# Tiles 4 to 9 of x laid out transposed by the host, their means spread by TensorE and subtracted by VectorE, and four weight slices moved to SyncE's queue

## The chip, the cores and the metric

The kernel runs on one core of one Trainium2 chip. The metric is the device time of one execution in microseconds (us). The arithmetic is f32; each f32 operand of a large product is split into a high part in the fp32r format and a low part, and three products (high x high, high x low, low x high) are summed, so that precision is kept.

## The reference, cut to what matters

x has 1250 rows (nodes) of 1024 features; there are 41,250 edges of two relations. Two layers, each with a residual:

```python
h = relu(layernorm(x))                        # rows
n = lnw * h * rsqrt(mean(h * h) + 1e-6)
y = elu(n @ W_root + bias + sum_r mean_over_edges_r(n @ W_rel[r]))
x = x + h + y @ wo
h = relu(layernorm(x)) @ W_gat                # second layer
e = exp(-leaky_relu(h @ a_l [src] + h @ a_r [dst]))
x = x + elu(scatter_sum(e * h[dst]) / (scatter_sum(e) + 1e-5))
```

The part that the change touches is the left operand of `n @ [W_rel, W_root]`: relu(layernorm(x)), transposed.

## The kernel before

The rows of x are worked in ten tiles of 125 (`TILES`, `T`), the 1024 features in eight slices of 128 (`KT`). Each engine has its own program, and semaphores tie them together; `data(t)` is the count that a semaphore has when tile t's data are there, `room(t)` and `room1(t)` the counts at which a buffer or bank is free again. `pipeline` (L269) runs stages with lags, tile after tile. There is no scheduler: the order on each engine is what is written.

First stage (about 10 to 120 us). For tile t: SyncE loads the rows into `xt` (`load_x`, L298). VectorE takes mean and variance (`variance`, L896; `moments`, L892) and the reciprocal of the deviation (`deviation`, L906). ScalarE normalises and takes relu in one instruction into `ht` (`norm`, L499) and the root of the mean square (`mean_square`, L506). GpSimd adds h to x (`residual`, L436) and SyncE stores the sum (`store_xh`, L303). TensorE turns the eight slices of `ht` into two PSUM banks (`transposed`, L1350; 8 transposes), ScalarE copies them out as `hT_hi` (`transposed`, L519), VectorE takes the rest as `hT_lo` = PSUM - `hT_hi` (`low_parts`, L917). TensorE then makes 48 products of the tile (`products`, L1358, by `split_products`, L1324), which ScalarE and VectorE scale by `stats1[..., 5]` and split into messages (`messages`, L536 and L934). The last tile's products (`last_products`, L1400) are mixed with the first counting matmuls.

```python
            def stage1(first, end):                                                     # TensorE, L1390
                pipeline((transposed, 1), (products, 2), steps=(first, end))
            def stage1(first, end):                                                     # VectorE, L974
                pipeline((transposed, 1), (messages, 2), (moments, -1), steps=(first, end))
```

So in a step VectorE does the low parts of one tile, the messages of the tile before, and the moments of a tile ahead. Between its steps it prepares the edges, one piece per step (L997 to L1012): `quotients` (L830), `listed` (L836), `picks` (L844), `spans_of_windows` (L859), then `window_keys` (L877) and `first_rows` (L970). TensorE needs them in its own queue: `picked` (L1331) stands behind the products of tile 5 and waits for the picks, `windows_transposed` (L1338) behind those of tile 7, `total` (L1346) behind those of tile 8. GpSimd's gather (L453) waits for the spans, and tile 8's residual stands behind it.

The passage to the second layer (about 230 to 260 us). SyncE's loop over tiles (L376) stores tile t's x1, then loads tile t + 2 of x + h (`load_xh`, L345), which waits until the store of the same buffer has ended; slice 0 of the second layer's weights is in that loop too (L383). ScalarE issues slices 1 to 3 behind the copy of slice 0 (L763) and slices 4 to 7 behind a change of its function table (`back_to_exp`, L767), ahead of `turned(TILES - 1, 0)` (L770), the first copy of the last tile's counts out of PSUM. TensorE's third counts transposition of that tile (L1669) waits for this copy. ScalarE and VectorE split the slices into `wg` (L641, L1093), and the products of tile 0 take them one after another (`products2`, L1563).

## Time and profile before

| | us |
|---|---|
| median of three runs | 515.79 (515.06 to 517.19) |
| the profiled execution, whole | 514.97 |
| its span, first to last instruction | 513.2 |
| TensorE busy in it | 495.4 |
| VectorE, ScalarE, GpSimd busy | 374.9, 226.7, 74.7 |
| mean granted clock of TensorE | 0.998 |

The profile names an instruction by its line in the program, its engine (PE is TensorE, PEld its weight loads, DVE VectorE, ACT ScalarE, POOL GpSimd, SPq SyncE's queue) and by output <- inputs. Matmuls overlap one another, so what one costs its engine is the distance from its start to the next one's start. "idle before" is the time in which the engine had nothing to do before an instruction, and the arrow names whose work ended it.

### The profile page before, as it was taken

What the parts mean: (1) busy time and instruction counts of PE and PEld (TensorE: products, weight loads), DVE (VectorE), ACT (ScalarE), POOL (GpSimd) and SP (SyncE); (2) the same over time, 40 slices, a digit from 0 to 9 for tenths busy, and PEclk for the clock granted to TensorE, in tenths of its full rate; (3) what the DMA queues carried; (4) which work ended last, traced back from release to release, by engine and by line L of the source; (5) the groups of instructions that cost most, each with busy time, mean ns of one, the idle gap of its engine ahead of it and who ended that gap; (6) DMA issues with size and microseconds to landing.
All of it is one profiled execution on the core that took longest, in us unless ns stands there. A gap on an engine that the chain in (4) does not pass through costs nothing.

```text
span 513.2 us, 7812 instructions
## 1 busy us (share of the span) xinstructions
PE 495.4 (97%) x2983; PEld 426.2 (83%) x2983; DVE 374.9 (73%) x644; ACT 226.7 (44%) x382; POOL 74.7 (15%) x72
## 2 busy tenths in 40 slices
PE   3999999999999999999999999999999999999996
PEld 2889989988989988898788888888887888888886
DVE  4846885598889999997865555556598878777633
ACT  5865443415966666667632222224233333223211
POOL 1362213100000000000000000000083333322400
PEclk9999999999999999999999999999999999999999
DMA  9872273404013235247911111100022222222211
GB/s 259 228 239 81 80 228 117 127 1 114 2 47 112 84 99 143 81 123 277 319 53 40 41 41 41 41 0 0 1 80 82 83 90 69 81 80 81 70 53 44
DMA packets 22186, 49.15 MB, mean 96 GB/s; under 512 B 4798, under 2 KB 10709, under 8 KB 22018
## 3 DMA queue, kind: packets, MB, share of 16 engines
q1 hardware_dynamic: 20879, 44.66, 29.2%
q10 hardware_dynamic: 1008, 3.67, 2.0%
q8 instruction: 26, 0.43, 0.4%
q0 software_dynamic: 256, 0.26, 0.2%
q14 instruction: 17, 0.14, 0.1%
HBM read 33.05 MB, written 16.85 MB: 97 GB/s over the span
## 4 chain that ended last, share of the span: by engine, by line
PE 86%; DVE 7%; DMA 4%; ACT 2%; issue 1%; SPq 0%; ACTq 0%; DVEq 0%
PE ps L1328 11%; PE ps L1593 9%; PE ps L1595 9%; PE ps L1594 9%; PE ps L1487 8%; PE ps L1574 7%; PE ps L1575 7%; PE ps L1576 7%; PE ps L1397 4%; PE ps L1416 2%; DMA x_scratch<-xt 1%; PE ps L1546 1%; DMA xt<-xh_scratch 1%; PE ps L1560 1%; PE ps L1548 1%; PE ps L1547 1%
## 5 line engine op out<-in xcount | busy, mean ns | idle before, releaser
L1593 PE MATMUL ps<-h_hi,att_hi 125*125 125x512 f32 (+1 forms) x190 | 73.5, 387 | 0.0
L1594 PE MATMUL ps<-h_lo,att_hi 125*125 125x512 f32 (+1 forms) x190 | 72.6, 382 | 0.0
L1595 PE MATMUL ps<-h_hi,att_lo 125*125 125x512 f32 (+1 forms) x190 | 72.5, 382 | 0.0
L1574 PE MATMUL ps<-wg,gT_hi 128*125 128x512 f32 x160 | 63.8, 399 | 0.3 <-DVE wg L1097 0.3
L1575 PE MATMUL ps<-wg,gT_hi 128*125 128x512 f32 x160 | 63.1, 394 | 0.0
L1576 PE MATMUL ps<-wg,gT_lo 128*125 128x512 f32 x160 | 63.0, 394 | 0.0
L1487 PE MATMUL ps<-msg_hi,adj_hi 125*125 125x288 f32 x180 | 50.3, 303 | 0.2 <-ACT adj_hi L596 0.2
L1487 PE MATMUL ps<-msg_lo,adj_hi 125*125 125x286 f32 x180 | 45.9, 295 | 0.0
L471 POOL TENSOR_TENSOR some<-first_att 125x625 f32<-125x625 f32 x1 | 2.4, 2440 | 277.8 <-DVE first_att L1157 277.8
L691 ACT ACTIVATE em<-ps,rinv 125x512 f32<-125x512 f32 (+1 forms) x21 | 14.0, 669 | 64.2 <-DVE hp L1201 64.2
L1595 PEld LDWEIGHTS ps<-h_hi,att_lo 125*125 125x125 f32 x190 | 35.2, 186 | 7.9
L1594 PEld LDWEIGHTS ps<-h_lo,att_hi 125*125 125x125 f32 x190 | 35.2, 185 | 7.5
L1593 PEld LDWEIGHTS ps<-h_hi,att_hi 125*125 125x125 f32 x190 | 35.2, 185 | 7.4
L1328 PE MATMUL ps<-w_hi,hT_hi 128*125 128x430 f32 x112 | 40.7, 363 | 0.5 <-DVE hT_lo L920 0.5
L1328 PE MATMUL ps<-w_hi,hT_lo 128*125 128x430 f32 x112 | 40.1, 358 | 0.0
L1328 PE MATMUL ps<-w_lo,hT_hi 128*125 128x430 f32 x112 | 40.0, 357 | 0.0
L1135 DVE CUSTOM_DVE_ANT_0 h_lo<-ps,a_b 125x1024 fp32r<-125x1024 f32 x20 | 24.5, 1224 | 18.1 <-PE ps L1576 17.7
L1574 PEld LDWEIGHTS ps<-wg,gT_hi 128*125 128x125 f32 x160 | 29.7, 186 | 7.7 <-DVE wg L1097 0.7
L1576 PEld LDWEIGHTS ps<-wg,gT_lo 128*125 128x125 f32 x160 | 29.6, 185 | 7.3
L1575 PEld LDWEIGHTS ps<-wg,gT_hi 128*125 128x125 f32 x160 | 29.7, 186 | 6.9
L668 ACT CAST h_hi<-ps 125x1024 fp32r<-125x1024 f32 x10 | 10.2, 1016 | 55.4 <-DVE diag L1139 55.4
L596 ACT CAST adj_hi<-ps 125x500 fp32r<-125x500 f32 x45 | 26.7, 592 | 16.2 <-PE ps L1397 15.5
(215 smaller groups left out, 1116.6 us busy)
## 6 DMA issues: line engine op xcount, KB each, us to landing
xt<-in_x SPq DMA_DIRECT2D x10, 448.0 KB
xh_scratch<-xt SPq DMA_DIRECT2D x10, 448.0 KB
xt<-xh_scratch SPq DMA_DIRECT2D x10, 448.0 KB
x_scratch<-xt SPq DMA_DIRECT2D x10, 448.0 KB
x1t<-x_scratch SPq DMA_DIRECT2D x10, 448.0 KB
xr<-x_scratch SPq DMA_DIRECT2D x10, 448.0 KB
out_x<-xr SPq DMA_DIRECT2D x19, 224.0 KB
wg_raw<-in_L_gnn_W ACTq DMA_DIRECT2D x7, 512.0 KB, 7.4
```

Source lines behind the costliest of these rows:

```text
L596: A.copy(columns(adj_hi, b, g), bank_of).then_inc(S["win_out"], 1)
L691: A.activation(em[b][:, first:end], heads(b, h, (first, end)), ACT.Exp, scale=rinv[b][:, 0:1]).then_inc(S["el_rdy"], 1)
L1135: V.tensor_tensor_reduce(out=halves(h_lo[:, TILES - 1, :]), in0=hps, in1=halves(a_b[:, s, :]), scale=1.0, scalar=0.0, op0=ALU.mult, op1=AL ...
L1328: last = M.matmul(out, lhsT, rhs, start=(n == 0), stop=(n == len(terms) - 1))
L1397: last = M.matmul(win_bank(n, x), srcs, wide, start=c == 0, stop=c == SLOTS - 1)
L1487: last = M.matmul(*product, start=(s == 0 and n == 0), stop=(end and n == 1), skip_group_check=True)
L1574: M.matmul(to, hi, wg[k][:, 0, cut], start=n == 0, stop=False)
L1575: M.matmul(to, hi, wg[k][:, 1, cut], start=False, stop=False)
L1576: last = M.matmul(to, lo, wg[k][:, 0, cut], start=False, stop=n == KT - 1)
L1593: M.matmul(to, hi[:, s, :], h_hi[:, s, cut], start=s == 0, stop=False)
L1594: M.matmul(to, hi[:, s, :], h_lo[:, s, cut], start=False, stop=False)
L1595: return M.matmul(to, lo[:, s, :], h_hi[:, s, cut], start=False, stop=s == TILES - 1)
```

## The change

The host hands x over a second time as `x_turned`, ten tiles with the features along the partitions (128 x 8 x 125). SyncE loads tiles 4 to 9 of it into two new buffers `x_t` (`load_x_turned`). For these tiles TensorE no longer transposes `ht`. `means` multiplies the column of the tile's means, broadcast over 128 columns, by the identity: one matmul puts the mean of each row into every partition of a bank. VectorE subtracts it from `x_t` (`centred`), ScalarE takes relu of that as `hT_hi` (`high_parts`), and VectorE takes the low part from `x_t` and `hT_hi` (`turned_low_parts`). The rows are no longer scaled by the reciprocal deviation at this place; it goes into the factor of the messages (`mean_square`). `norm` and the sum x + h stay as they are. Tile 3 keeps its transposes. Apart from that, weight slices 4 to 7 are issued by SyncE ahead of `load_x1(2, 0)`, and no longer by ScalarE.

```diff
+    TURNED = 4
...
+    XT_AT = (2 * TILES * N - 2 * 4 * KT * T) // 32 * 32
...
+        turned_of = ExitStack()
+        sb(turned_of, "below_x_t", [P, XT_AT // 2], BF16)
+        x_t = [sb(turned_of, f"x_t{b}", [P, KT, T], F32) for b in range(2)]
+        turned_of.close()
...
+            def load_x_turned(t, b):
+                if t >= TURNED + 2:
+                    sp.wait_ge(S["hT_lo_rdy"], data(t - 2))
+                sp.dma_start(x_t[b][:], x_turned[t].rearrange("p (k n) -> p k n", n=T)).then_inc(S["xt_in"][b], 16)
...
             load_x(5, 1)
+            load_x_turned(4, 0)
+            load_x_turned(5, 1)
             store_xh(2, 0)
             store_xh(3, 1)
...
                 store_xh(t, t % 2)
                 if t + 2 < TILES:
                     load_x(t + 2, t % 2)
+                if TURNED + 2 <= t + 1 < TILES:
+                    load_x_turned(t + 1, (t + 1) % 2)
...
                 if t == TILES - 2:
+                    sp.wait_ge(S["s_ps"], data(TILES - 1))
+                    for k in range(4, KT):
+                        load_wg(k)
                     load_x1(2, 0)
                 store_x1(t, t % 2)
...
             def norm(t, b):
                 act.wait_ge(S["rstd_rdy"], data(t))
-                act.wait_ge(S["hT_ps"], room(t))
+                if t < TURNED + 2:
+                    act.wait_ge(S["hT_ps"], room(t))
                 act.wait_ge(S["xh_rdy"], room(t))
                 A.activation(ht[b][:], xt_of(t)[:], ACT.Relu, bias=stats1[:, bass.ds(t, 1), 3],
...
+            def high_parts(t, b):
+                act.wait_ge(S["centred"], t - TURNED + 1)
+                act.wait_ge(S["g_ps"], room(t))
+                A.activation(hT_hi[b][:], x_t[b][:], ACT.Relu).then_inc(S["hT_hi_rdy"], 1)
...
-            pipeline((transposed, 1), (messages, 2), (normed, -1), steps=(AHEAD, TILES + 1))
+            transposed(3, 1, 1)
+            for t in range(AHEAD, TILES):
+                messages(t - 2, t % 2, t // 2 - 1)
+                high_parts(t, t % 2)
+                if t + 1 < TILES:
+                    normed(t + 1, 1 - t % 2, (t + 1) // 2)
+            messages(TILES - 2, 0, TILES // 2 - 1)
...
                 if k == 1:
                     act.wait_ge(S["sum_16"], data(TILES - 1))
-                if k == 4:
-                    act.wait_ge(S["s_ps"], data(TILES - 1))
                 act.dma_start(wg_raw[k][:], w_gat[k * P:(k + 1) * P, :]).then_inc(S["wg_in"][k], 16)
...
                 back_to_exp()
-                for k in range(4, KT):
-                    load_wg(k)
                 turned(TILES - 1, 0)
                 elu(*last)
                 turned(TILES - 1, 1)
...
             def mean_square(t):
+
                 dve.wait_ge(S["rm_rdy"], data(t))
-                V.reciprocal(stats1[:, bass.ds(t, 1), 5], stats1[:, bass.ds(t, 1), 5]).then_inc(S["rms_rdy"], 1)
+                last = V.reciprocal(stats1[:, bass.ds(t, 1), 5], stats1[:, bass.ds(t, 1), 5])
+                if t >= TURNED:
+                    last.then_inc(S["rs1_rdy"], 1)
+                    dve.wait_ge(S["rs1_rdy"], t - TURNED + 1)
+                    last = V.tensor_tensor(stats1[:, bass.ds(t, 1), 5], stats1[:, bass.ds(t, 1), 5], stats1[:, bass.ds(t, 1), 2], ALU.mult)
+                last.then_inc(S["rms_rdy"], 1)
+
+            def centred(t, b):
+                dve.wait_ge(S["xt_in"][b], (t - b) * 8 + 16 - 8 * TURNED)
+                dve.wait_ge(S["mean_ps"], t - TURNED + 1)
+                V.tensor_tensor(x_t[b][:], x_t[b][:], bank(b, P, T).unsqueeze(1).broadcast_to([P, KT, T]), ALU.subtract).then_inc(S["centred"], 1)
+
+            def turned_low_parts(t, b):
+                dve.wait_ge(S["hT_hi_rdy"], data(t))
+                V.scalar_tensor_tensor(hT_lo[b][:], x_t[b][:], 0.0, hT_hi[b][:].bitcast(F32), ALU.max, ALU.subtract).then_inc(S["hT_lo_rdy"], 1)
...
-            def stage1(first, end):
-                pipeline((transposed, 1), (messages, 2), (moments, -1), steps=(first, end))
+            def step1(t):
+                centred(t, t % 2)
+                messages(t - 2, t % 2, t // 2 - 1)
+                turned_low_parts(t, t % 2)
+                mean_square(t)
+                if t + 1 < TILES:
+                    moments(t + 1, 1 - t % 2, (t + 1) // 2)
 
             dve.wait_ge(S["consts"], 1)
...
-            stage1(AHEAD, 5)
+            transposed(3, 1, 1)
+            step1(4)
             quotients()
-            stage1(5, 6)
+            step1(5)
             listed()
-            stage1(6, 7)
+            step1(6)
             picks()
-            stage1(7, 8)
+            step1(7)
             spans_of_windows()
-            stage1(8, 9)
-            stage1(9, 10)
+            step1(8)
+            step1(9)
             window_keys()
             first_rows(range(0, 2))
-            stage1(10, 11)
+            messages(TILES - 2, 0, TILES // 2 - 1)
             missing()
             first_rows(range(2, 2 * NG))
-            stage1(11, 12)
+            messages(TILES - 1, 1, TILES // 2 - 1)
...
+            def means(t):
+
+                b = t % 2
+                pe.wait_ge(S["var_rdy"], data(t))
+                if t >= TURNED + 2:
+                    pe.wait_ge(S["centred"], t - TURNED - 1)
+                else:
+                    pe.wait_ge(S["hT_lo_rdy"], data(TURNED - 1 if TURNED < AHEAD else TURNED - 2))
+                M.matmul(bank(b, P, T), mv[b][:, 0:1].broadcast_to([T, P]), ident[0:T, 0:T], start=True, stop=True).then_inc(S["mean_ps"], 1)
+
             def stage1(first, end):
-                pipeline((transposed, 1), (products, 2), steps=(first, end))
+                for t in range(first, end):
+                    products(t, t % 2, t // 2)
+                    if t + 2 < TILES:
+                        means(t + 2)
...
-            stage1(AHEAD, 8)
+            transposed(3, 1, 1)
+            stage1(2, 6)
             picked()
-            stage1(8, 10)
+            stage1(6, 8)
             windows_transposed()
-            stage1(10, 11)
+            stage1(8, 9)
             total()
             last_products()
...
+    laid = {name: inputs[name] for name in INS}
+    laid["x_turned"] = np.asarray(inputs["x"]).reshape(10, 125, 8, 128).transpose(0, 3, 2, 1).reshape(10, 128, 1000)
+    for name in [INS[0], "x_turned"] + INS[1:]:
+        a = np.ascontiguousarray(laid[name])
```

VectorE, the step ahead of the picks (`picks` begins at the CAST into `qb`); `hT_lo` is a tile's low parts, `bn` and `mv` the moments of tile 7. Before:

```order
L920 TENSOR_TENSOR hT_lo<-ps,hT_hi 128x500 x2
L932 RECIPROCAL stats<-stats 125x1
L943 SCALAR_TENSOR_TENSOR root<-ps,stats,bias_b 125x286
L945 SCALAR_TENSOR_TENSOR msg_lo<-ps,stats,msg_hi 125x572
L823 BN_STATS bn<-xt 125x6 x2
L904 BN_AGGR mv<-bn 125x2
L908 RECIPROCAL stats<-stats 125x1
L910 SCALAR_TENSOR_TENSOR stats<-mv,stats 125x1
L848 CAST qb<-quot 110x3x125
```

Now:

```order
L969 TENSOR_TENSOR x_t<-x_t,ps 128x1000
L984 SCALAR_TENSOR_TENSOR root<-ps,stats,bias_b 125x286
L986 SCALAR_TENSOR_TENSOR msg_lo<-ps,stats,msg_hi 125x572
L973 SCALAR_TENSOR_TENSOR hT_lo<-x_t,hT_hi 128x1000
L959 RECIPROCAL stats<-stats 125x1
L963 TENSOR_TENSOR stats<-stats 125x1
L849 BN_STATS bn<-xt 125x6 x2
L930 BN_AGGR mv<-bn 125x2
L934 RECIPROCAL stats<-stats 125x1
L936 SCALAR_TENSOR_TENSOR stats<-mv,stats 125x1
L874 CAST qb<-quot 110x3x125
```

The centring stands at the head of the step, the low parts have moved behind the messages, and a second scale instruction has come; all of it is ahead of the picks. The low parts in this step were tile 5's and are tile 6's now, the messages are tile 4's in both.

TensorE, the end of tile 5's products (L1328, now L1375) and what follows. Before:

```order
L1328 MATMUL ps<-w_lo,hT_hi 125x430
L1328 MATMUL ps<-w_hi,hT_lo 125x430
L1335 MATMUL ps<-qb,pick 125x127 x6
L1355 MATMUL ps<-ident,ht 128x125 x8
L1328 MATMUL ps<-w_hi,hT_hi 125x430
```

Now:

```order
L1375 MATMUL ps<-w_lo,hT_hi 125x430
L1375 MATMUL ps<-w_hi,hT_lo 125x430
L1445 MATMUL ps<-ident,mv 128x125
L1382 MATMUL ps<-qb,pick 125x127 x6
L1375 MATMUL ps<-w_hi,hT_hi 125x430
```

The matmul that spreads a mean (tile 7's here) comes before the six of `picked`, and tile 6's products follow them at once; the eight transposes are gone.

ScalarE in the passage, from the table change on. Before:

```order
L576 ACT_TABLE_LOAD
L576 ACTIVATE ssq<-eps 125x1
L639 DMA wg_raw<-in_L_gnn_W 128x1024 x4
L616 CAST counts<-ps 125x500
L621 ACTIVATE eb<-eb 125x286
```

Now:

```order
L684 ACTIVATE x1t<-x1t,stats 125x1024
L607 ACT_TABLE_LOAD
L607 ACTIVATE ssq<-eps 125x1
L647 CAST counts<-ps 125x500
L652 ACTIVATE eb<-eb 125x286
```

The four DMAs have left the place ahead of the copy of counts; in SyncE's queue they stand between the load of tile 9 of x + h and that of `x1t` for tile 2.

## Rows read from the trace of the kernel before

**Rows 1.** The page's busy table: engine, busy us, share of span, instructions.

```profile
PE 495.4 (97%) x2983; PEld 426.2 (83%) x2983; DVE 374.9 (73%) x644; ACT 226.7 (44%) x382; POOL 74.7 (15%) x72
```

**Rows 2.** Waits of TensorE: engine, line, for whom, us in total, times, longest.

```profile
PE ps L1514 <- ACT counts L616: 1.0, 1, 1.0
...
PE ps L1574 <- DVE wg L1097: 0.3, 1, 0.3
```

**Rows 3.** Timeline of TensorE: start us, busy us, line, output<-inputs, form, count.

```profile
44.10 1.02 PE L1355 MATMUL ps<-ident,ht 125*128 125x125 f32 x8
44.88 0.43 PE L1328 MATMUL ps<-w_hi,hT_hi 128*125 128x430 f32 x1
...
54.38 1.04 PE L1355 MATMUL ps<-ident,ht 125*128 125x125 f32 x8
```

**Rows 4.** Timeline of TensorE at 282 us, second layer.

```profile
282.34 0.38 PE L1584 MATMUL ps<-diag,ones 125*125 125x125 f32 x2
282.56 0.91 PE L1560 MATMUL ps<-ident,x1t 125*128 125x125 f32 x7
```

**Rows 5.** Timeline of VectorE, 45 to 75 us, first stage.

```profile
45.07 0.52 DVE L943 SCALAR_TENSOR_TENSOR root<-ps,stats,bias_b 125x286 f32<-125x286 f32 x1 [1.94 <-ACT msg_hi L539]
...
46.22 1.28 DVE L823 BATCH_NORM_STATS2 bn<-xt 125x6 f32<-125x512 f32 x2
...
48.49 0.74 DVE L832 CAST edges_f<-edges_i 110x1125 f32<-110x1125 int32 x1
...
49.66 0.36 DVE L828 TENSOR_SCALAR quot<-quot 110x375 f32<-110x375 f32 x1
50.05 2.50 DVE L827 TENSOR_SCALAR quot<-edges_f 110x375 f32<-110x375 f32 x1
...
52.97 1.26 DVE L920 TENSOR_TENSOR hT_lo<-ps,hT_hi 128x500 fp32r<-128x500 f32 x2
...
58.70 0.54 DVE L838 SCALAR_TENSOR_TENSOR comb<-quot,edges_f 110x375 f32<-110x375 f32 x1
...
63.57 1.26 DVE L920 TENSOR_TENSOR hT_lo<-ps,hT_hi 128x500 fp32r<-128x500 f32 x2
...
69.11 0.55 DVE L848 CAST qb<-quot 110x375 bf16<-110x375 f32 x1
...
74.84 1.25 DVE L920 TENSOR_TENSOR hT_lo<-ps,hT_hi 128x500 fp32r<-128x500 f32 x2
```

**Rows 6.** Timeline of GpSimd, the residual of tile 5.

```profile
49.94 2.40 POOL L438 TENSOR_TENSOR xt<-ht,xt 125x1024 f32<-125x1024 f32 x1 [9.18 <-ACT ht L503]
```

**Rows 7.** Groups of VectorE by line and form: count, busy us, mean ns, idle.

```profile
L1153 DVE SCALAR_TENSOR_TENSOR first_att<-first_att 125x1000 f32<-125x1000 f32 x1 | 1.2, 1199 | 0.0
```

**Rows 8.** Timeline of TensorE, the picks' matmuls and tile 6's products.

```profile
75.22 0.51 PE L1335 MATMUL ps<-qb,pick 110*125 110x127 bf16 x6
...
77.05 0.44 PE L1328 MATMUL ps<-w_hi,hT_hi 128*125 128x430 f32 x1
```

**Rows 9.** Timeline of TensorE, its first matmuls.

```profile
8.68 1.93 PE L1385 MATMUL ps<-ident,ht 125*128 125x125 f32 x8 [3.26 <-ACT ht L503]
...
12.92 1.02 PE L1355 MATMUL ps<-ident,ht 125*128 125x125 f32 x8
```

**Rows 10.** Stretches after TensorE's end: length, busy us by engine, granted clock, DMA.

```profile
508.50:509.00 0.50, 0.28 (x3) 0.07 (x1) 0.18 (x1) 0.00 (x0) 0.00 (x0) 1.00 0.07 10
...
511.00:511.50 0.50, 0.00 (x0) 0.00 (x0) 0.00 (x0) 0.00 (x0) 0.00 (x0) 0.71 0.50 141
```

**Rows 11.** Timeline of ScalarE, the copy of the last tile's counts.

```profile
238.48 0.58 ACT L616 CAST counts<-ps 125x500 uint16<-125x500 f32 x1 [1.27 <-issue]
```

**Rows 12.** Chain that ended last, 234 to 249 us: start, us, what.

```profile
234.30 7.49 DMA x_scratch<-xt
...
242.15 7.01 DMA xt<-xh_scratch
```

**Rows 13.** The weight slices' DMAs: us to landing, shortest, median, longest.

```profile
DMA to landing us min/median/max: 3.6/7.0/10.2
```

10 lines of the change are left out of this document (4 added, 6 removed).

## The prediction

> **What bounds the kernel now.** I read the page's busy table first. TensorE is busy for 495.4 of 513.2 us [rows 1], so almost every microsecond of its queue is on the path, and a change pays only by taking work or waits out of that queue. Then I asked who TensorE waits for [rows 2]: once it has started, its waits are short, and two of them lie where this change works: 1.0 us for a ScalarE copy of counts and 0.3 us for the last slice of the second layer's weights. So I read two places as timelines. In the first stage (34 to 108 us) TensorE goes from tile to tile without a gap; VectorE has about as much to do there, because four pieces of edge preparation (quotients, list, picks, spans) stand between its tiles. In the passage from the first layer to the second (234 to 257 us) the chain of waits leaves TensorE and runs through a store, a load and VectorE.
>
> One execution was profiled: 514.97 us, of which 513.2 are the span. The median of the three runs is 515.79. The sum below is a difference, worked out on the profiled execution and added to the median. A measurement of this kernel can tell about 0.5% (2.6 us) from no change.
>
> **TensorE, per tile.** For tiles 4 to 9 the eight transposes go. They begin at 44.10 and the next product begins at 44.88 [rows 3]: 0.78 us. What comes in their place is one small matmul with a broadcast operand. The nearest row is the matmul that spreads the diagonal in the second layer, 0.22 us from start to start [rows 4]. That leaves 0.56 us a tile, 3.4 us over six, if nothing else ends later. A tile's 48 products take 9.50 us (44.88 to 54.38) [rows 3], so the period falls from 10.28 to 9.72 us.
>
> **VectorE, per tile.** Before, a step is low parts (two instructions), messages, moments. Now it is centring, messages, low parts, two tiny scale instructions, moments. Prices from the rows of this stage: messages 1.15 us (45.07 to 46.22), moments 2.27 (46.22 to 48.49) [rows 5]. The new low part has two operands of 1000 columns in SBUF; the same instruction on 125x1000 took 1.20 us [rows 7], of which the start of the next overlaps a little: 1.15. The centring has one operand in PSUM; no row shows it with a broadcast, and by the 1000 columns of [rows 7] it lies between 1.1 and 1.3: 1.15. Scales 0.27. Sum 6.0 us, where the step before had 4.8. The 1.2 us more are hidden only while VectorE has slack in that period, and it has none in three steps in a row: after tile 4 the quotients follow (48.49 to 52.97, 4.48 us), after tile 5 the list (58.70 to 63.57, 4.87), after tile 6 the picks (69.11 to 74.84, 5.73) [rows 5].
>
> Followed through: the mean of tile 4 is spread when the products of tile 2 end, so step 4 starts at about 44.4. It ends with its quotients at 44.4 + 6.0 + 4.48 = 54.9. Step 5 with the list ends at 54.9 + 6.0 + 4.87 = 65.8. Step 6 with the picks ends at 65.8 + 6.0 + 5.73 = **77.5**, where it ended at 74.84 before. The centring stands at the head of VectorE's step, so messages, low parts, moments and the preparation all queue behind it.
>
> Who waits for the picks: TensorE's six `picked` matmuls, which stand behind the products of tile 5, as before. TensorE now gets there earlier: 44.10 + 0.22, then three periods of 9.50 and 0.22, is 73.5 us. It waits **4.0 us**, where before it came at 75.22 and found the picks done [rows 8]. It can't go round them: the products of tile 6 stand behind `picked` in its queue. They start at 77.5 + 0.5 = 78.0 instead of 77.05 [rows 8], 0.9 us late. All that tiles 4 to 7 had won is gone. Tiles 8 and 9 give back 2 x 0.56. The first stage ends **0.2 us earlier**. By an error of 0.1 us in each of the six new large instructions this is off by 0.6 either way.
>
> Covered, with the cover named. The low parts of tile 7 are done at 77.5 + 3.5 = 81, and its products can't start before 87.5; tiles 8 and 9 have more. The window keys come 2 us closer to their use and still before it. ScalarE loses 2 copies of 500 columns and gains one of 1000. SyncE's queue takes six more loads of 500 KB; the tightest is tile 8's, which stands behind the list's spans and tile 9's rows; it is wanted at 88, and low parts 6 us later still come before TensorE asks for them.
>
> **The clock.** TensorE's last matmul ends at 508.78; the granted clock is still full until 511 and 0.71 in the half microsecond after it, so it fell to its lower level (1.2 of 2.4 GHz) about 2.4 us after the engine stopped [rows 10]. A stop of 4.0 us in mid-kernel is longer. What it costs is read from the start, where TensorE came out of idleness: eight transposes took 1.93 us at 8.68, and the next eight, at 12.92, 1.02 [rows 9]. So the price is between 0.9 us (those transposes alone) and 2.1 (half of the 4.2 us in between); no row decides, and I take 1.2, nearer the lower, since the level may rise before 12.92. The Trainium skill, "TensorE: Matmul & The Clock Gate", section "HAM oscillation", speaks against this change in the same way: a matmul kernel that idles between bursts comes back at half rate each time. By that the gain of the change is eaten here; without it the sum is 1.2 us lower.
>
> **The passage to the second layer.** ScalarE issued the four slices itself, and the copy of counts behind them starts at 238.48 after 1.27 us of "issue" [rows 11]. TensorE waits 1.0 us for that copy [rows 2]. With the issues gone the copy runs at 237.2; TensorE goes on at 238.0 with eight transposes and then waits for y of the last tile, which needs ScalarE's exponential of the same stretch and comes 0.6 us earlier. So of 1.0 us, **0.6** stays. SyncE issues the slices behind its load of tile 9, and that load waits for the store of tile 7, which took 7.49 us; the load then took 7.01 and landed at 249.16 [rows 12], with slices on the other queue moving beside both. Without four of them the store ends no later and the load has the engines for itself; in half its time it would be there at 245.7, and VectorE would no longer wait for it. Its splits then run 1 to 2 us ahead, and the **0.3** us [rows 2] that TensorE stood at the last slice goes too. Sum **0.9 us earlier**; between 0, if the slices now come late, and 1.3, all of both waits.
>
> **The sum:** -0.2 - 0.9 + 1.2 = +0.1; 515.79 + 0.1 = **515.9 us**, no change that can be measured. Nothing later in the kernel depends on either place except through TensorE's queue.
>
> **Rivals.**
> 1. *The clock stays up.* For it: one fall in the trace, at the end, isn't a rule for a stop of 4 us, and the small matmul of the mean and the six of the picks fall near its ends. Then the sum is -1.1: 514.7 us.
> 2. *VectorE is in time.* If its step were short enough for the picks at 73.5, TensorE would save all: products of tile 6 at 74.0 instead of 77.05, then 1.1, then 0.9: -5.05, 510.7 us. Against it: 4 us would have to be missing from 35 us of VectorE rows. It decides from picks before 75 us.
> 3. *VectorE meets GpSimd.* GpSimd's residual add starts at 49.94 and takes 2.40 us [rows 6]. The VectorE instruction that runs into it, at 50.05, took 2.50 us, where the one before it, of the same kind and shape, took 0.36 [rows 5]: 2.1 us lost. Before, low parts read one operand from PSUM; now both are in SBUF. If the add falls on them in steps 4 to 6, the picks come 3 x 2.1 = 6.3 us later still, and all of that is TensorE's: 522 us. Against it: the add begins 1.45 us after the moments end and is over by 3.9, in the middle of the preparation, while the next low part starts at 6.8 at the earliest; it decides if the add is delayed by 3 us. Only tile 8's, which stands behind the gather, can meet one, with 5 us of slack. The Trainium skill, "SBUF — State Buffer", section "Who interferes with whom", has the rule: a VectorE instruction with two SBUF inputs is blocked in full by a GpSimd one that reads SBUF. By that rule alone each new low part is at risk; by the rows none on the path is.
> 4. *The slices come late.* One took 10.2 us to land at most [rows 13]; issued at 244.1 it would land at 254.3, be split by 256.5, with ScalarE's and VectorE's copies: TensorE would go on when it did before, and of the 0.9 us nothing is left, 516.8 us. Against it: four slices of 512 KB alone on the engines have no rival traffic but one load.
>
> **Chances.** The forecast, stall and slow clock, 0.45 (515.9, and 515 to 517 by its bounds). The stall without the clock 0.25 (514.7). VectorE in time, or the stall under 2 us, 0.14 (510.7 to 513). GpSimd or another delay of over 2.6 us 0.11. Late slices 0.05. Faster by over 0.5% means below 513.2: 0.16, with a little from the second case's lower end. Slower by over 0.5%, above 518.4: 0.12. Within: 0.72. The range runs from 510.5 to 518.5: it takes in rival 2, and leaves out the GpSimd case and little more.
>
> **What would show it.** Right: VectorE's picks end near 77.5; TensorE shows one wait of 3.5 to 4.5 us on them; the granted clock is below 1 around 76 to 80 and the products there take twice as long; the first stage's last products start within 0.5 us of before, plus what the clock cost; the wait on the counts copy is gone. Wrong: picks before 75 us, a low part of over 2 us, a centring over 1.4, or TensorE waiting on `x_t` loads or on the slices.

## The result and the profile after

| | before | changed |
|---|---|---|
| median of six runs each | 515.94 | 518.93 (517.64 to 519.32) |
| ratio to before | 1 | 1.0049, interval 1.0035 to 1.0064 |
| the profiled execution, whole | 514.97 | 518.34 |
| its span | 513.2 | 516.1 |
| mean granted clock | 0.998 | 0.995 |

The changed kernel is slower by 0.49%, 2.5 us (1.8 to 3.3). The forecast was 515.9 with a range of 510.5 to 518.5; 1.0049 x 515.79 is 518.3, inside the range by 0.2 us (the changed kernel's own median of 518.93 is above it). "No change that can be measured" holds by a hair only: the loss is under the 0.5% that the forecast named, but it is clear of the noise, and the forecast's middle was 2.4 us too low. The first stage came out as forecast and the passage did not, so that the time still fell into the range is partly luck.

TensorE's busy time in the page fell as it should, and the span grew:

```profile
PE 492.4 (95%) x2947; PEld 424.0 (82%) x2947; DVE 382.3 (74%) x650; ACT 227.4 (44%) x376; POOL 74.7 (14%) x72
```

That is 3.0 us less work [rows 1] and 2.9 us more span. TensorE's waits (engine, line, for whom, us in total, times, longest) say where the work's place was taken:

```profile
PE ps L1382 <- DVE pick L882: 4.3, 1, 4.3
...
PE ps L1635 <- DVE wg L1144: 2.0, 1, 2.0
```

The first is the stall that the forecast named. The second is 2.0 where it was 0.3 [rows 2], and the forecast had it gone. The wait of 1.0 on the counts [rows 2] is gone; 0.6 us on y, behind it, is what was left of it.

**First stage.** VectorE's timeline of the changed kernel (start, busy us, line, output<-inputs, form, count): a step with the quotients behind it (L853), one with the list (L867), and the step with the picks (L879, L882).

```profile
44.27 1.20 DVE L969 TENSOR_TENSOR x_t<-x_t,ps 128x1000 f32<-128x1000 f32 x1 [0.99 <-PE ps L1445]
...
46.57 1.20 DVE L973 SCALAR_TENSOR_TENSOR hT_lo<-x_t,hT_hi 128x1000 fp32r<-128x1000 f32 x1
...
51.00 0.35 DVE L853 TENSOR_SCALAR quot<-edges_f 110x375 f32<-110x375 f32 x1
...
51.78 2.51 DVE L853 TENSOR_SCALAR quot<-edges_f 110x375 f32<-110x375 f32 x1
...
54.72 1.20 DVE L969 TENSOR_TENSOR x_t<-x_t,ps 128x1000 f32<-128x1000 f32 x1
...
62.41 2.63 DVE L867 SCALAR_TENSOR_TENSOR comb<-comb,edges_f 110x375 f32<-110x375 f32 x1
...
65.54 1.19 DVE L969 TENSOR_TENSOR x_t<-x_t,ps 128x1000 f32<-128x1000 f32 x1
...
73.02 2.94 DVE L879 TENSOR_SCALAR below<-iw,last_q 110x250 bf16<-110x250 f32 x3
75.99 1.26 DVE L882 SCALAR_TENSOR_TENSOR pick<-iw,most,below 110x250 bf16<-110x250 f32 x3
77.17 1.19 DVE L969 TENSOR_TENSOR x_t<-x_t,ps 128x1000 f32<-128x1000 f32 x1
```

Centring and low part take 1.20 us each and 1.1 from start to start. Step 4 with the quotients lasts 10.45 (44.27 to 54.72; forecast 10.48), step 5 with the list 10.82 (10.87), step 6 with the picks 11.63 (11.73). The picks end at 77.2. TensorE, a tile's period and the stall:

```profile
43.91 0.44 PE L1375 MATMUL ps<-w_hi,hT_hi 128*125 128x430 f32 x1
...
53.35 0.38 PE L1445 MATMUL ps<-ident,mv 125*128 125x125 f32 x2
53.49 0.44 PE L1375 MATMUL ps<-w_hi,hT_hi 128*125 128x430 f32 x1
...
72.61 0.38 PE L1445 MATMUL ps<-ident,mv 125*128 125x125 f32 x2
77.30 0.90 PE L1382 MATMUL ps<-qb,pick 110*125 110x127 bf16 x6 [4.31 <-DVE pick L882]
77.97 0.70 PE L1375 MATMUL ps<-w_hi,hT_hi 128*125 128x430 f32 x1
78.47 0.56 PE L1375 MATMUL ps<-w_lo,hT_hi 128*125 128x430 f32 x1
...
88.65 0.38 PE L1445 MATMUL ps<-ident,mv 125*128 125x125 f32 x2
```

This tile takes 9.58 us (43.91 to 53.49), where the forecast had 9.72 and the kernel before 10.28: the mean's matmul costs 0.14 here, not 0.22, and the 48 products of tile 3 took 9.44, not 9.50. Over all six tiles the transposes cost 0.77 to 0.81 us each before, and the means cost 0.14 to 0.22: about 0.62 us saved per tile. TensorE had spread the mean of tile 7 by 73.0, waited 4.31 us, and did tile 6's products in 10.68 us (77.97 to 88.65) where 9.50 is the full-clock time [rows 3]. The picks' matmuls took 0.67 us from the first to the products behind them; at full clock they take 0.37 (the run with a filler, below). The clock beside it, in stretches of 1 us (length, busy us of PE, PEld, DVE, ACT, POOL with instructions, granted clock, DMA share, GB/s):

```profile
76.00:77.00 1.00, 0.00 (x0) 0.00 (x0) 1.00 (x3) 0.00 (x0) 0.00 (x0) 1.00 1.03 359
77.00:78.00 1.00, 0.70 (x7) 0.70 (x7) 1.00 (x2) 0.00 (x0) 0.00 (x0) 0.55 1.05 361
...
79.00:80.00 1.00, 1.00 (x5) 0.91 (x4) 1.00 (x2) 0.42 (x1) 0.00 (x0) 0.50 0.99 383
...
81.00:82.00 1.00, 1.00 (x7) 0.95 (x6) 1.00 (x2) 0.00 (x0) 0.00 (x0) 1.00 0.13 53
```

The clock is at half speed (1.2 GHz) from shortly before TensorE resumes until about 80.5.

**The passage.** The chain of waits of the changed kernel (start, us, what):

```profile
245.63 10.10 DMA x1t<-x_scratch
...
255.82 1.30 DVE bn L849 x2
...
257.46 1.10 DVE wg L1144
```

Before, the chain went through the load of tile 9 of x + h [rows 12]. Now it goes through SyncE's queue (four slices are issued from 243.06 on) to the load of x1 for tile 2 behind them, 10.10 us, then VectorE's moments of that tile, then the last slice's split, then TensorE. Two more views:

ScalarE's timeline, the changed kernel:

```profile
237.89 0.56 ACT L647 CAST counts<-ps 125x500 uint16<-125x500 f32 x1
...
254.64 1.05 ACT L672 CAST wg<-wg_raw 128x1024 fp32r<-128x1024 f32 x1 [1.50 <-DMA wg_raw<-in_L_gnn_W]
```

VectorE's timeline, the changed kernel:

```profile
255.82 1.29 DVE L849 BATCH_NORM_STATS2 bn<-x1t 125x6 f32<-125x512 f32 x2 [1.42 <-DMA x1t<-x_scratch]
...
257.38 1.17 DVE L1144 TENSOR_TENSOR wg<-wg_raw,wg 128x1024 fp32r<-128x1024 f32 x1
```

The copy of counts starts 0.12 us after the table change, with no issue ahead of it. But ScalarE now waits for each of the four slices to land, 3.5 us in all, and VectorE's last split starts at 257.38, where it started at 255.35.

**Where the time went.** The beginning of an execution varies: the products of tile 2 start at 34.56 and 35.49 us in two traces of the kernel before and between 34.2 and 36.3 in the others, whether or not they have the transposed tiles. This is probably much of the spread of the runs. So two stretches are compared between fixed events of TensorE: (A) from the products of tile 2 to the first counting product, (B) from there to the second layer's first broadcast (the matmul on `diag`).

| trace | A | B | runs against before, % |
|---|---|---|---|
| before, first trace | 87.24 | 148.32 | |
| before, second trace | 87.23 | 148.85 | |
| changed | 88.37 | 149.53 | +0.49 (0.35 to 0.64) |
| slices alone | 87.24 | 149.06 | +0.12 (-0.05 to 0.30) |
| transposed tiles alone | 88.44 | 150.08 | +0.70 (0.47 to 0.93) |
| filler in the stall | 87.07 | 149.21 | +0.11 (-0.02 to 0.25) |
| picked behind tile 6 | 86.18 | 149.25 | +0.05 (-0.11 to 0.21) |
| slices early | 89.17 | 149.98 | +0.92 (0.65 to 1.20) |
| last split first | 88.36 | 148.60 | +0.51 (0.31 to 0.72) |
| preparation early | 83.82 | 148.59 | -0.28 (-0.46 to -0.11) |
| the same, keys and split too | 84.39 | 149.08 | -0.24 (-0.41 to -0.08) |
| before, preparation early | 87.39 | 148.24 | +0.04 (-0.11 to 0.20) |
| before, one more input in DRAM | 87.24 | 148.93 | -0.11 (-0.23 to 0.02) |
| preparation early, slices on ScalarE | 83.87 | 149.63 | -0.37 (-0.53 to -0.21) |

0.1% is 0.5 us. A repeats to 0.1 us wherever the code of the stage and the clock are the same. B does not: with the same code of the passage it is 148.2 to 148.9 in four traces without the transposed tiles, and 149.6 and 150.1 in two with them.

One part of the time is in neither stretch. The whole execution is longer than its span, by 1.76 to 1.94 us in every run whose span is on record without the transposed tiles (with an unread input too), and by 2.13 to 2.32 us in every one with them. So 0.4 us of what the transposed tiles cost lies outside the span; what it is was not looked for.

### The profile page after: what moved, and what is told of

It reads as the page before. It is cut to its first block, busy times and chain, and to the rows that moved or that the text cites. A ratio compares the mean times of both kernels' runs of the same rounds, so it can differ in the third digit from the quotient of the medians.

```text
span 516.1 us, 7751 instructions
## 1 busy us (share of the span) xinstructions
PE 492.4 (95%) x2947; PEld 424.0 (82%) x2947; DVE 382.3 (74%) x650; ACT 227.4 (44%) x376; POOL 74.7 (14%) x72
## 4 chain that ended last, share of the span: by engine, by line
PE 81%; DVE 10%; DMA 4%; ACT 2%; issue 2%; SPq 1%; ACTq 0%; DVEq 0%
PE ps L1654 9%; PE ps L1655 9%; PE ps L1656 9%; PE ps L1548 8%; PE ps L1375 8%; PE ps L1635 7%; PE ps L1636 7%; PE ps L1637 7%; PE ps L1457 4%; DMA x1t<-x_scratch 2%; DVE bn L849 2%; PE ps L1476 2%; PE ps L1607 1%; PE ps L1621 1%; DMA x_scratch<-xt 1%
## 5 line engine op out<-in xcount | busy, mean ns | idle before, releaser
L1375 PE MATMUL ps<-w_hi,hT_hi 128*125 128x430 f32 x112 | 41.3, 369 | 0.4 <-DVE hT_lo L946 0.4
L1375 PE MATMUL ps<-w_hi,hT_lo 128*125 128x430 f32 x112 | 40.5, 362 | 0.0
L1375 PE MATMUL ps<-w_lo,hT_hi 128*125 128x430 f32 x112 | 40.4, 361 | 0.0
L696 ACT CAST h_hi<-ps 125x1024 fp32r<-125x1024 f32 x10 | 10.2, 1016 | 55.4 <-DVE diag L1186 55.4
```

Of the source, the lines that this page charges most:

```text
L1375: last = M.matmul(out, lhsT, rhs, start=(n == 0), stop=(n == len(terms) - 1))
```

## The experiments

All are edits of the changed kernel unless they say otherwise.

### Slices alone (an edit of the kernel before)

```diff
                 if t == TILES - 2:
+                    sp.wait_ge(S["s_ps"], data(TILES - 1))
+                    for k in range(4, KT):
+                        load_wg(k)
                     load_x1(2, 0)
...
                 back_to_exp()
-                for k in range(4, KT):
-                    load_wg(k)
                 turned(TILES - 1, 0)
```

> The kernel before, with the slices of the second layer's weights numbered 4 to 7 issued by SyncE behind its load of tile 9 of x + h, and nothing else changed. The forecast said 0.9 us less: about 515.0, with the last slice ready by 255.5 and no wait of TensorE on it. The trace of the changed kernel says the opposite: the slices are issued 6 us later, the load of x1 for tile 2 stands behind them and lands late, VectorE's moments wait for it, and the last split stands behind these: TensorE resumes 1.2 us later, about 517.1 us. If neither holds and the passage was late only because the first stage shifted it, the time stays at 515.9.

Measured: +0.12% (-0.05 to 0.30), +0.6 us. The forecast's 0.9 us less (-0.17%) lies outside the interval. From the first counting product to the first product with the new weights it is 123.98 us, against 124.48 and 124.58 in the two traces before: 0.5 to 0.6 gained at the copy of counts, as forecast. From there to the broadcast it is 25.08, against 23.84 and 24.27: 0.8 to 1.2 lost. The mechanism is that of the changed kernel:

The chain of waits, the slices alone:

```profile
246.31 9.13 DMA x1t<-x_scratch
255.53 1.30 DVE bn L822 x2
```

TensorE's waits, the slices alone:

```profile
PE ps L1573 <- DVE wg L1096: 1.5, 1, 1.5
```

ScalarE waits for the slices here too, 1.29 us for the first of the four and 1.35 for the last. So the slices' move makes this loss without any transposed tile, and its gain and loss nearly cancel. The gain repeats: up to the first product with the new weights it is 124.5 to 125.0 us in all six traces with the slices on ScalarE's queue, and 124.0 in seven of the eight with them on SyncE's (124.8 in the run with the filler).

### Transposed tiles alone

```diff
                 if t == TILES - 2:
-                    sp.wait_ge(S["s_ps"], data(TILES - 1))
-                    for k in range(4, KT):
-                        load_wg(k)
                     load_x1(2, 0)
...
                 back_to_exp()
+                for k in range(4, KT):
+                    load_wg(k)
                 turned(TILES - 1, 0)
```

> The changed kernel with the four slices back on ScalarE's queue, so the transposed tiles alone. If the two parts add up, the first stage ends 0.8 us later than in the kernel before (stall of 4.3 us, slow clock 1.3, against six transpositions saved) and the passage is as before: 516.8 us, with TensorE's wait of 1.0 us on the counts back and its wait on the last slice at 0.3. If the slices' cost came from the first stage's shift, 518.9 as in the changed kernel.

Measured: +0.70% (0.47 to 0.93), +3.6 us, where about +1.0 was expected. A is 1.20 us longer than before: the first stage's loss is all the transposed tiles'. B is 1.2 to 1.8 longer although its code is that of before: the load of tile 9 of x + h took 9.10 us, and TensorE waited 0.9 us for a middle slice, 0.5 for the last and 1.5 for the counts. Neither alternative had waits of this size. The time is nearer to the second, but a later start of the passage doesn't explain it: B is long in the last run too, where the passage starts earlier than before. The next two runs and the last one ask what it is.

### The kernel before, again

> The kernel before, unchanged, for a second trace of it. Its first trace and the run with the slices alone back on ScalarE have the same code in the passage, but the load of tile 9 of x + h took 7.0 us in the one and 9.1 in the other, and the passage from the first counting product to the second layer's first broadcast 148.3 and 150.1 us. If that is variation from one execution to the next, this trace shows 149 to 150 us too (and the first trace was a quick one). If the transposed tiles cause it, it shows 148.3 +- 0.3 again.

Measured: one run of 516.98. A is 87.23, B 148.85, half a microsecond more than the first time. TensorE waited 1.18 and 0.46 us at the two places of [rows 2] and not at all at a middle slice. So B varies, but not by as much as in the run above.

### Before, with an input that nothing reads

```diff
-def rgcn_gat_kernel(nc, x, src,
+def rgcn_gat_kernel(nc, x, x_turned, src,
```

Here `x_turned` is laid out and handed over as in the changed kernel.

> The kernel before with x_turned as one more input in DRAM that nothing reads. With the slices on ScalarE's queue the stretch from the first counting product to the second layer's first broadcast took 148.2 to 148.9 us in three traces without the transposed tiles and 149.6 and 150.1 in two with them, although no instruction of that stretch differs. If the extra input alone does it (5 MB more, so that the buffers behind it lie elsewhere), this trace shows 149.5 or more and the median is about 1 us above before. If it is the loads and instructions of the transposed tiles, or variation between executions, the trace shows 148.2 to 148.9 and the median stays within 0.8 us of before.

Measured: -0.11% (-0.23 to 0.02), B 148.93. The extra input is not the cause. What B follows is one transfer, the load of tile 9 of x + h. The chains of waits of the kernel before's second trace and of the transposed tiles alone:

The chain of waits, the kernel before's second trace:

```profile
242.92 7.70 DMA xt<-xh_scratch
```

The chain of waits, the transposed tiles alone:

```profile
243.92 9.10 DMA xt<-xh_scratch
```

In the five traces with this code in which it is on the chain it took 7.01 [rows 12], 7.70, 7.84 (this run), 8.40 (preparation early, slices on ScalarE) and 9.10 us, and B was 148.32, 148.85, 148.93, 149.63 and 150.08. In the same five traces the slowest slice landed 10.2, 11.2, 11.3, 11.8 and 13.1 us after its issue, in the same order, with the DMA engines full (a share of 1.0) while the load runs: the transfers of the stretch are slow together, not this load alone. That is a ranking in five traces; no run tested it. Why they are slowest in the two with transposed tiles was not found: it isn't the stall, since one of the two has none.

This bears on the changed kernel as well. Its B is 0.7 to 1.2 us longer than in the kernel before, and the slices' move and this unexplained part could each have made that; the single traces don't divide it between the two.

### A filler in the stall

```diff
             def picked():
+                for n in range(20):
+                    M.matmul(bank(6, T, FB), w_hi[:, n % KT, 0, 0:T], w_hi[:, n % KT, 1, :], start=True, stop=True)
                 pe.wait_ge(S["picks_rdy"], 1)
```

> The changed kernel with 20 matmuls of 128x430 on constant operands ahead of TensorE's wait for the picks; their result is overwritten and used by nobody. They fill about 3.9 of the 4.3 us of the stall, so VectorE's part of the loss stays and only the idleness goes. If the granted clock falls because TensorE stands still, it stays at 1.0 now: the picks' matmuls take 0.5 us in place of 0.67 and tile 6's products 9.5 in place of 10.68, 1.35 us in all, and the time is 518.9 - 1.35 = 517.6 us. If something else takes the clock down there (the DMA traffic, the small matmuls), the products of tile 6 still take 10.7 us and the time stays at 518.9.

Measured: +0.11% (-0.02 to 0.25), 2.0 us (0.38%) less than the changed kernel, 1.3 by A (87.07 against 88.37). TensorE's timeline and the clock:

TensorE's timeline, the filler:

```profile
74.77 4.13 PE L1380 MATMUL ps<-w_hi 128*125 128x430 f32 x20
79.41 0.56 PE L1384 MATMUL ps<-qb,pick 110*125 110x127 bf16 x6 [0.50 <-DVE pick L882]
79.78 0.44 PE L1375 MATMUL ps<-w_hi,hT_hi 128*125 128x430 f32 x1
```

Stretches, the filler:

```profile
79.00:80.00 1.00, 0.59 (x7) 0.59 (x8) 1.00 (x2) 0.00 (x0) 0.00 (x0) 1.00 0.89 279
80.00:81.00 1.00, 1.00 (x6) 0.95 (x6) 1.00 (x3) 0.51 (x1) 0.00 (x0) 1.00 1.02 329
```

The picks come as late as ever, the real work resumes as late, and yet the products of tile 6 take 9.51 us (79.78 to 89.29). The DMA engines are as busy beside it (a share of 0.88 to 1.16 from 74 to 80), so what took the clock down was that TensorE stood still; work that nobody uses was faster here than waiting.

### The picks' matmuls behind tile 6

```diff
-            stage1(2, 6)
+            stage1(2, 7)
             picked()
-            stage1(6, 8)
+            stage1(7, 8)
```

> The changed kernel with the six matmuls of picked moved behind the products of tile 6. If the stall on the picks is what ate the gain, the wait of 4.3 us and the slow clock behind it (1.2 us on tile 6's products, 0.2 on the picks' matmuls) both go, VectorE's spans start at 83.7 where they started at 83.1, and the time is 518.9 - 5.6 = 513.3 us. If another wait takes its place (the windows' gather, the window keys, total), TensorE stands there instead and the time is above 515. If VectorE's six costlier steps bound the stage by themselves, it stays near 518.9.

Measured: +0.05% (-0.11 to 0.21), 2.3 us (0.44%) less than the changed kernel, not 5.6. The stall is gone, and three waits have taken its place:

```profile
PE ps L1445 <- DVE mv L930: 1.5, 1, 1.5
PE ps L1395 <- DVE found L911: 0.9, 1, 0.9
...
PE ps L1457 <- DVE ring L1008: 0.5, 1, 0.5
```

2.9 us, for the moments of tile 9, the count of found windows and the ring's first row. All are at VectorE's end: TensorE's order is not the limit, VectorE's queue is.

### The preparation one step earlier

```diff
+            quotients()
             messages(1, 1, 0)
             transposed(3, 1, 1)
             step1(4)
-            quotients()
+            listed()
             step1(5)
-            listed()
-            step1(6)
             picks()
+            step1(6)
             step1(7)
```

> The changed kernel with VectorE's preparation of the edges one step earlier: quotients before the messages of tile 1, in the 3.4 us that VectorE idles there, list and picks each a step earlier. TensorE's order is untouched. If VectorE's queue is what ends last at the picks, they are ready at about 67, TensorE goes from tile 5 to 6 without a wait and at full clock, the changed kernel's 4.3 + 1.35 us go and the time is 518.9 - 5.6 = 513.3 us; no wait on the window keys should take their place, since VectorE's later steps come earlier too. If GpSimd's sum (38.5 to 40.9 us) blocks a quotient for its whole 2.4 us, the products of tile 3 start up to 0.5 us later. If the six costlier VectorE steps bound the stage themselves, waits on the low parts appear and the time is above 516.

Measured: -0.28% (-0.46 to -0.11), 1.4 us faster than before and 4.0 faster than the changed kernel. A is 83.82, 3.42 us less than before. That adds up: the six transposes' places give 3.75 us, the wait of 0.5 us on tile 6's low parts went as well, 0.6 came from the products of tiles 3 and 4, the picks' and the windows' matmuls, and the two new waits, of 1.2 us, took back 1.45 from start to start. Two timelines:

VectorE's timeline, the preparation early:

```profile
39.00 2.51 DVE L853 TENSOR_SCALAR quot<-edges_f 110x375 f32<-110x375 f32 x1
...
66.24 1.26 DVE L882 SCALAR_TENSOR_TENSOR pick<-iw,most,below 110x250 bf16<-110x250 f32 x3
```

TensorE's timeline, the preparation early:

```profile
73.26 0.38 PE L1445 MATMUL ps<-ident,mv 125*128 125x125 f32 x2
73.48 0.51 PE L1382 MATMUL ps<-qb,pick 110*125 110x127 bf16 x6
```

One quotient meets GpSimd's sum and takes 2.51 us, which VectorE could afford; the picks are ready at 67.5, and TensorE goes through. Of the expected 5.6 us against the changed kernel, A shows 4.55; TensorE now waits 0.73 us for found windows and 0.48 for the ring, which was expected not to come. A and B together say 3.2 us or more less than before, the runs 1.4 (0.6 to 2.4). B was a quick one in this trace (148.59, against 149.1 to 150.1 in seven of the eight others with the transposed tiles), and 0.4 us came outside the span. With a B of 149.1 to 150.1 the traces give 1.2 to 2.8 us less, which the interval of the runs overlaps.

### Control: the same in the kernel before

```diff
+            quotients()
             messages(1, 1, 0)
             stage1(AHEAD, 5)
-            quotients()
+            listed()
             stage1(5, 6)
-            listed()
-            stage1(6, 7)
             picks()
+            stage1(6, 7)
             stage1(7, 8)
```

> The kernel before, with nothing but the preparation of the edges one step earlier on VectorE: the control for that move. In the kernel before VectorE had the picks 0.4 us ahead of TensorE, and the only wait near it is 0.5 us on tile 6's low parts behind them. If the move only undoes the stall that the change brought, it is worth 0.5 us here, 0.1%. If an early preparation is worth as much without the transposed tiles as with them (3.9 us), the gain of that run is not a matter of the change at all.

Measured: +0.04% (-0.11 to 0.20), A 87.39 against 87.24. The move is worth nothing without the transposed tiles. The 0.5 us at tile 6's low parts went, and 0.9 came for those of tiles 4 and 5, which now stand behind quotients and list.

### Slices ahead of the load of tile 9

```diff
                 if t == TILES - 2:
-                    sp.wait_ge(S["s_ps"], data(TILES - 1))
-                    for k in range(4, KT):
-                        load_wg(k)
                     load_x1(2, 0)
                 store_x1(t, t % 2)
+                if t == TILES - 3:
+                    sp.wait_ge(S["s_ps"], data(TILES - 1))
+                    for k in range(4, KT):
+                        load_wg(k)
```

> The changed kernel with the four slices still in SyncE's queue, but between the store of x1 of tile 7 and the load of tile 9 of x + h, so that they are issued as soon as the counts are summed (about 237 to 239) and the load of x1 for tile 2 is no longer behind them. If the place in SyncE's queue is what costs 1.2 us, the cost goes and the 0.3 to 0.9 us of the relieved counts copy and last slice come: 516.8 to 517.4 us. If four slices beside the store of tile 7 delay that store, and so the load of tile 9 and VectorE behind it, the time is 518 or more.

Measured: +0.92% (0.65 to 1.20), worse than the changed kernel. The load of tile 9 of x + h is back on the chain, and VectorE waits 3.57 us for it:

The chain of waits, the slices early:

```profile
244.46 9.16 DMA xt<-xh_scratch
```

VectorE's timeline, the slices early:

```profile
253.71 1.22 DVE L1130 TENSOR_TENSOR xt<-ps,xt 125x1024 f32<-125x1024 f32 x1 [3.57 <-DMA xt<-xh_scratch]
```

Stretches, the slices early:

```profile
244.00:248.00 4.00, 4.00 (x19) 3.01 (x18) 3.62 (x7) 4.00 (x6) 0.00 (x0) 1.00 1.03 415
...
252.00:256.00 4.00, 2.43 (x11) 1.61 (x9) 2.29 (x3) 3.00 (x3) 0.00 (x0) 1.00 1.04 334
```

The store of tile 7 was not delayed (6.79 us); the load was. The DMA engines are full from 244 to 256 (in the changed kernel too, 0.87 to 1.06 in stretches of 4 us), so the slices probably compete with loads that are wanted at the same time, and whatever goes first makes the rest late. The transposed tiles alone had a load of 9.10 us too, so this trace doesn't show how much of the 9.16 the slices' place made. A is 0.8 us longer than in the changed kernel with the same code: the clock fell earlier in the stall here (0.79 in the microsecond from 76 to 77) and was back at 83.4, 4.9 us after TensorE had resumed, where it took 3.2 in the changed kernel. The granted clock of the six runs is 0.988 to 0.995, against 0.993 to 0.997 in the changed kernel's six, so part of the +0.92% is the stall's clock and not the slices.

### The last split ahead of the moments

```diff
-                variance2(2, 0)
                 split_gat_weights(range(7, KT))
+                variance2(2, 0)
                 deviation2(2, 0)
```

> The changed kernel with VectorE's moments of tile 2 of the second layer moved behind its split of the last weight slice. In the changed kernel that split started at 257.4 us though ScalarE had the slice's high part at 255.7: the moments, which wait until 255.8 for the load of x1 that stands behind the four slices in SyncE's queue, were ahead of it. If that order is what makes TensorE wait 2.0 us, the wait falls to about 0.3 and the time to 517.2 us. If the slices' own landing is what ends last, the wait shrinks by under 0.5 us and the time stays above 518.4.

Measured: +0.51% (0.31 to 0.72), as the changed kernel. TensorE no longer waits for the split, but it waits 1.23 us for the normalised x1, whose moments now come behind the split; B is 0.9 shorter in the trace, and the medians do not show it. The run says nothing certain about the time. It moves the wait, and shows that the order of two VectorE instructions is not by itself what bounds the passage.

### Everything together

The preparation early, with

```diff
-            step1(9)
             window_keys()
+            step1(9)
```

and the last split first.

> The changed kernel with the preparation of the edges one step earlier (as in the run before), and also the window keys ahead of VectorE's step of tile 9, and VectorE's moments of tile 2 of the second layer behind the split of the last slice. With the stall on the picks gone, TensorE waited 0.73 us for the count of found windows and 0.48 for the first row of the ring. If the place of the keys behind step 9 causes these, both go and the time is 1.2 us below the last run's; the order of the last split was worth 0.9 us in the trace of its own run, though nothing in the medians. So 1.2 to 2.1 us below that run: against the kernel before, -2.6 to -3.5 us. If the low parts of tile 9, now behind the keys, come late instead, TensorE waits for them before its last products and the gain is 0 or less.

Measured: -0.24% (-0.41 to -0.08), no better than the preparation alone. The wait on found windows went; 0.70 us for tile 9's low parts and 0.75 for the ring came, and one of the keys' instructions met GpSimd:

VectorE's timeline, everything together:

```profile
94.58 2.50 DVE L899 TENSOR_SCALAR kk<-kk 128x500 f32<-128x500 f32 x1
```

GpSimd's timeline, everything together:

```profile
94.40 2.40 POOL L457 TENSOR_TENSOR xt<-ht,xt 125x1024 f32<-125x1024 f32 x1 [4.96 <-ACT ht L523]
```

2.50 us, where the same instruction took 0.42 in the changed kernel.

### The preparation early, slices on ScalarE's queue

> The changed kernel with the preparation one step earlier and the four slices back on ScalarE's queue, to see the slices' move once more, beside a first stage that has no stall. Before against slices alone gave +0.6 us for the move, turned alone against both gave -1.1; both are within what five rounds tell. If the move is worth nothing either way, this is within 0.7 us of the run with the preparation early (-1.4 us against the kernel before). If the slices in SyncE's queue are late and cost 1.2 us, this is 1.2 us faster than that; if they relieve ScalarE by the forecast's 0.9, it is 0.9 slower.

Its edit is that of the run with the preparation early and that of the transposed tiles alone. Measured: -0.37% (-0.53 to -0.21), 1.9 us faster than before (1.1 to 2.7). With the slices in SyncE's queue it was -0.28%; the intervals overlap by most of their width. With the preparation at its old place it was +0.70% on ScalarE's queue and +0.49% on SyncE's, and without transposed tiles 0 and +0.12%. None of the three pairs is told apart: the move of the slices is worth about 0.2% at most, in whichever direction.

## Why the forecast was right and wrong

- **VectorE bounds, picks late, TensorE stands.** Right in mechanism, place and size. The forecast had the picks end at 77.5 and a stall of 4.0 us; measured were 77.2 and 4.3. Set from the products of tile 2, which started 0.3 earlier here, the picks are 0.02 us off. The new large instructions were priced at 1.15 and cost 1.1. The run with the preparation early shows that this queue, and not the new work as such, cost the time.
- **0.56 us a tile.** Right in kind, a little small: it is 0.62 on average, and all of it came as soon as VectorE let it.
- **The clock.** Right in mechanism, a little small: 1.2 us was forecast from the first transposes, and 1.18 on the products and 0.30 on the picks' matmuls (0.67 against 0.37) were measured, 1.5 together; A of the filler's run is 1.3 lower. In the run in which the clock stayed low for longer, slices early, it was 1.96 + 0.29, just above the upper end of 2.1 that had been given. The forecast's 0.5 us for the picks' matmuls at full clock was too long by 0.13 from start to start, which hid part of this. By the Trainium skill, "TensorE: Matmul & The Clock Gate", section "HAM oscillation", a kernel that idles between bursts comes back at half rate: the traces of the changed kernel and of slices early agree (0.50 as TensorE resumes), while with the transposed tiles alone it came back at 1.00 and fell to 0.50 within the next microsecond.
- **The first stage's sum**, -0.2 + 1.2 = +1.0: measured +1.13 by A.
- **The passage, -0.9: wrong.** The step that failed is "Its splits then run 1 to 2 us ahead, and the 0.3 us that TensorE stood at the last slice goes too". The copy of counts gave its 0.5 to 0.6, as forecast. But the slices are issued from 243 on, where ScalarE had issued them at 236 to 238. The forecast knew this (rival 4 has 244.1) and still let the splits run ahead. And the load of x1 for tile 2, which the forecast never looked at, stands behind them in the same queue. It took 10.1 us, VectorE's moments waited for it in front of the last split, and TensorE's wait grew from 0.3 to 2.0. The forecast had "without four of them the store ends no later and the load has the engines for itself" and followed only the load ahead of the slices (it did come in time), not the one behind. What stands behind a new entry was asked for VectorE's queue and not for SyncE's. Rival 4 had the right sign and half of the mechanism (the last slice lands at 254.6, it had 254.3), with a chance of 0.05 and a price of 0.9 us; the distance from the forecast was 1.6 to 2.1 in the traces. How much of that is the slices' and how much the slower transfers that came with the transposed tiles is open; slices alone, by its runs, is 0.6 to 2.4 us above the -0.9.
- **Rival 3, VectorE meets GpSimd.** No low part on the path met an add, as judged. The forecast counted one meeting in the rows, in the quotients, and didn't ask what it costs VectorE's queue. There is one in each of the three crowded steps, in the changed kernel as in the kernel before, each on a preparation instruction:

GpSimd's timeline, the changed kernel:

```profile
72.94 2.34 POOL L457 TENSOR_TENSOR xt<-ht,xt 125x1024 f32<-125x1024 f32 x1 [8.31 <-ACT ht L523]
```

The adds of the other two steps start at 51.66 and 62.12. One quotient takes 2.51 us where its twin at 51.00 took 0.35, one instruction of the list 2.63 where those beside it took 0.55, and the first of the three `below` of the picks 2.4 of their 2.94: about 2.1 us each, 6.3 together, which is more than the stall of 4.3. They are inside the 4.48, 4.87 and 5.73 us that the forecast took from the rows, so its sum is right with them. No run moved the adds and the preparation apart; what that would give is not shown.

A low part can be hit as well. In the run with the preparation early that of tile 8 falls on GpSimd's add, while in the changed kernel a centring does.

VectorE's timeline, the preparation early:

```profile
88.61 2.12 DVE L973 SCALAR_TENSOR_TENSOR hT_lo<-x_t,hT_hi 128x1000 fp32r<-128x1000 f32 x1
```

GpSimd's timeline, the preparation early:

```profile
87.23 2.44 POOL L457 TENSOR_TENSOR xt<-ht,xt 125x1024 f32<-125x1024 f32 x1
```

VectorE's timeline, the changed kernel:

```profile
89.14 1.20 DVE L969 TENSOR_TENSOR x_t<-x_t,ps 128x1000 f32<-128x1000 f32 x1 [3.76 <-PE ps L1445]
```

GpSimd's timeline, the changed kernel:

```profile
88.64 2.43 POOL L457 TENSOR_TENSOR xt<-ht,xt 125x1024 f32<-125x1024 f32 x1
```

The low part, with two SBUF operands, takes 2.12 us in place of 1.20; the centring, with one operand in PSUM, takes its usual 1.20 beside the same add. By the Trainium skill, "SBUF — State Buffer", section "Who interferes with whom", a VectorE instruction with two SBUF inputs is blocked while a GpSimd one reads SBUF. The trace agrees for the low part: it starts at 88.61, the add ends at 89.67, and 1.06 + 1.1 is the time it took.

Together: +1.13 in A, +0.7 to +1.2 in B and +0.4 outside the span are 2.2 to 2.7 us, against 2.5 measured.

## What to carry to other kernels

Work taken from a full engine pays only if the engine that feeds it can keep the shorter period; if it can't, look for idle time ahead of the crowded steps and move its other work there, which here turned +0.5% into -0.3%. Price a stall of some microseconds on TensorE higher than its length, by what the clock costs afterwards: 1.5 to 2.3 us here, for 4.3 us. Look at which instructions of the crowded queue take several times what their twins take: here three of them stood behind GpSimd's adds. When a transfer moves into another queue, follow what stands behind it there and who waits for that, above all where the DMA engines are full: with the slices alone, leaving ScalarE's queue gave 0.5 to 0.6 us and cost 0.8 to 1.2 behind it, and in the runs the move was worth nothing that can be told.

## What the runs showed that was not expected

Twenty matmuls on constants, written over by the next real ones, made the kernel 2.0 us faster (1.3 by the trace). After the same stall of 4.3 us the clock was low for different times: back 3.2 us after TensorE resumed in the changed kernel and 4.9 us in the run with the slices early, which cost 1.18 and 1.96 us on the same products (10.68 and 11.46 us). And in the run with the transposed tiles alone it fell only after TensorE had resumed: 1.00 in the half microsecond from 78.49, 0.50 a microsecond later.
